# Two passes over the edges of a graph network: loops on the engines, or every quad written out

## The chip, the cores and the metric

The kernel runs on one core of one Trainium2 chip, in one launch. The metric is the device time of one execution in microseconds (us), lower is better. The engines go by their short names: PE (TensorE, its weight loads apart as PEld), DVE (VectorE), ACT (ScalarE), POOL (GpSimd) and SP (SyncE, which here only issues transfers). Each has its own stream of instructions, and they meet at semaphores.

## What is computed

Two layers of attention over a graph of 6250 nodes and 106,250 edges, each followed by a residual and a layer norm. The edges are sorted by destination. Cut to the work per edge:

```python
# layer 0: 8 heads of 16                       # layer 1: 4 heads of 32
Q, K, V = x @ Wq, x @ Wk, x @ Wv               x_src = x @ W_src + b_src; x_dst = x @ W_dst + b_dst
q = Q[dst] + rel_q[type]                       c = leaky_relu(x_src[src] + x_dst[dst] + emb[type], 0.2)
k = K[src] + rel_k[type] + time_emb @ Wt + bt  logits = einsum("ehd,hd->eh", c, att)
v = V[src] + rel_v[type]                       mx = segment_max(logits, dst)
euclid = sum(q * k, -1) / 4 * decay            ex = exp(logits - mx[dst])
dist = norm(m[src] - m[dst])                   attn = ex / segment_sum(ex, dst)[dst]
logits = a*euclid - (1-a)*beta*dist*decay      agg = segment_sum(x_src[src] * attn, dst)
ex = exp(logits - segment_max(logits, dst)[dst])   y = x + film(agg @ W_out + b_out)
agg = segment_sum(v * ex / segment_sum(ex, dst)[dst], dst)
x = norm(x + attention_block(agg))             x = norm(x + norm(y))
```

## The kernel before

The edges lie in tiles of 128, and nodes in blocks of 120. Where a tile spans two blocks it is worked through once for each, so there are 884 steps, and four steps make a quad: 221 quads with work (`sz.quads`; 224 by the padded count `NQUAD`). The program has six stages with barriers between them: `front` (schedule, tables), `edges0`, `join_tiles` with `nodes0`, `edges1`, `join_tiles`, `nodes1`. The change touches `edges0` and `edges1` alone.

In `edges0` every engine walks over the quads c = 0, 1, 2, ... in a function `emit` (on POOL `gather`). What one quad takes:

- POOL gathers the rows of the 4 x 128 source nodes with four indirect transfers (L1106) into a ring of 12 quads. It waits until the sums of the quad 12 before are made (L1103).
- PE multiplies the edge features (L1321), the queries (L1325) and the points (L1331, L1333), and, for the quad 8 before, the one-hot matrix with the weighted values (L1345, `sums`).
- DVE adds the times (L1161), multiplies by the queries (L1166), reduces per head (L1172), builds the transposed one-hot matrix of the quad 2 ahead (L1132) and the other one-hot matrix (L1180), scales the values (L1196), and adds four partial sums to the accumulator (L1150), whose block is read from a table into registers every fourth quad (a register load, L949). Once in four quads (a group, `LQ0`) it adds the distances (L1185, L1199) and one quad later makes the running maximum (L1190, L1204, L1211, L1215).
- ACT squares (L1283), copies the sums out of PSUM (L1275), and issues half of the feature loads; SP issues the rest and the loads by group.

`edges1` is built alike, with a ring of 16 quads, groups of eight, and a lag of ten quads between a quad's logits and its sums: POOL L1838, PE L2014, L2016 and L2040, DVE L1866 (transposed one-hot), L1879, L1884, L1888, L1895, L1898, L1908 (four adds), ACT L1981.

The order on each engine is that of the code. What the change concerns is how the quads are laid out in the program. Before, each engine has three stretches: a **head** written out, a **loop** whose body holds one turn of the ring, and a **tail** written out. In `edges0` the head is quads 0 to 23, the loop has 15 rounds of 12 quads (24 to 203), and the tail is the rest. In `edges1` the head is quads 0 to 31, the loop has 11 rounds of 16 quads (32 to 207). A loop of 15 rounds jumps back 14 times, and one of 11 rounds 10 times. In a body, the round is a register i, and each wait is for a number that depends on it; the helpers `nth0`, `group`, `slot` and `Chain.base` return a number where i is None and an expression of the register where it is not:

```python
def nth0(i, c, per=1, plus=0):
    v = c * per + plus
    return v if i is None else i * (RQ0 * per) + v
```

Of the kernel before, what the change touches and what calls it, by code (L numbers as in the profile page):

```python
# [39 lines left out]
LQ = 8  # L40
RQ = 16
# [3 lines left out]
LQ0, RQ0, LAG0, NQN = 4, 12, 7, 2  # L45
# [550 lines left out]
def tables0(nc, k, ctx):  # L596
# [4 lines left out]
    C = sz.steps // P  # L601
    PER = 2
    FROM = NGR - NBP // PER
    XT, FT = 6, 4
# [356 lines left out]
def edges0(nc, k):  # L961

    io, sz = k.io, k.sz
    NBP, S, T = sz.nbp, sz.steps, sz.tiles
    W = W0
    NQUAD = S // QS
    HEAD = 2 * RQ0
    NITER = (NQUAD - HEAD - LAG0 - 4) // RQ0
    TAIL = HEAD + NITER * RQ0
    PER = RQ0 * 7 + RQ0 // LQ0 * 5  # L970
    GS = LQ0 * QS
    BQ = 1
    with ExitStack() as ctx:
# [38 lines left out]
        vec = sem("vec")  # L1012
# [11 lines left out]

        def quads(i, c0, emit):
            for c in range(c0, c0 + (RQ0 if c0 else HEAD)):
                emit(i, c)

        def whole(eng, emit):
            quads(None, 0, emit)  # L1030
            with eng.Fori(0, NITER) as i:
                quads(i, HEAD, emit)
            for c in range(TAIL, NQUAD + LAG0 + 4):
                emit(None, c)

        with nc.Block() as block:
            @block.sync
            def _(sp):
# [50 lines left out]
                for c in range(5):  # L1089
                    load_feat(None, c)  # L1090
                whole(sp, emit)
                sp.wait_ge(zeroed, 64)
# [5 lines left out]
            def _(pl):  # L1098
# [11 lines left out]

                quads(None, 0, gather)
                with pl.Fori(0, NITER) as i:
                    quads(i, HEAD, gather)
                for c in range(TAIL, sz.quads):
                    gather(None, c)

            @block.vector
            def _(dve):
                V = nc.vector
                v = Chain(dve, vec)  # L1120
                V.memset(wbd[:, :, :], 0.0).then_inc(ready, 1)
                v.did(V.memset(acc, 0.0))
                count = {"base": v.n}
# [11 lines left out]
                def emit(i, c):  # L1135
                    w, a = c - LAG0, c - LAG0 - 2
                    v = Chain(dve, vec, count["base"] if i is None else i * PER + count["base"])
                    r = c % RQ0 * QS
# [84 lines left out]
                for j in range(k.sz.joins):  # L1223
                    if j % 16 == 0:
                        tiles = load_joins(nc, k, ET.DVE, 0, j, k.sz.etiles)
                    V.tensor_scalar(k.apart[:, j:j + 1], k.joinf[:, j:j + 1], k.entry[:, bass.ds(tiles[j % 16], 1)], None, ALU.subtract)
                quads(None, 0, emit)
                first = count["base"]
                with dve.Fori(0, NITER) as i:
                    quads(i, HEAD, emit)  # L1230
                assert count["base"] - first == PER, (count["base"] - first, PER)
                count["base"] = first + PER * NITER
                for c in range(TAIL, NQUAD + LAG0 + 4):
                    emit(None, c)

            @block.scalar
            def _(act):
# [65 lines left out]
                for c in range(5):  # L1303
                    load_feat(None, c)
                whole(act, emit)

            @block.tensor
            def _(pe):
# [52 lines left out]

                edge(None, 0)
                whole(pe, emit)


# [373 lines left out]
def edges1(nc, k):  # L1739

    io, sz = k.io, k.sz
    NBP, S = sz.nbp, sz.steps
    W = W1
    NQUAD = S // QS
    HEAD = 2 * RQ
    NITER = (NQUAD - HEAD) // RQ - 1
    PER = RQ * 6 + RQ // LQ * 2
    with ExitStack() as ctx:
# [32 lines left out]
        vec = sem("vec")  # L1781
        LAG = LQ + 2

        def quads(i, c0, emit):
            for c in range(c0, c0 + (RQ if c0 else HEAD)):
                emit(i, c)

        def whole(eng, emit):
            quads(None, 0, emit)
            with eng.Fori(0, NITER) as i:  # L1790
                quads(i, HEAD, emit)
            for c in range(NQUAD - RQ, NQUAD + LAG + 2):
                emit(None, c)
# [4 lines left out]
        with nc.Block() as block:  # L1798
            @block.sync
            def _(sp):  # L1800
# [21 lines left out]
                group_in(None, 0)  # L1822
                whole(sp, emit)
                chunks = math.ceil(sz.quads / 4)
# [4 lines left out]
            def _(pl):  # L1829
# [12 lines left out]

                quads(None, 0, gather)
                with pl.Fori(0, NITER) as i:
                    quads(i, HEAD, gather)
                for c in range(NQUAD - RQ, sz.quads):
                    gather(None, c)

            @block.vector
            def _(dve):  # L1850
                V = nc.vector
                v = Chain(dve, vec)
# [4 lines left out]
                pre = v.n  # L1857
# [10 lines left out]
                counted = {}  # L1868

                def emit(i, c):  # L1870
                    w, a = c - LAG, c - LAG - 1
                    g_u = c // LQ % 2
                    v = Chain(dve, vec, counted["base"] if i is None else i * PER + counted["base"])
                    if live(i, c + 2):
# [39 lines left out]
                    if maxing:  # L1914
                        u = m // LQ % 2
                        n = m // LQ // 2
# [17 lines left out]
                    if live(i, a):  # L1934
                        v.settle()
                        dve.sem_inc(added, 1)
                    counted["n"] += v.n
                    counted["base"] = counted["base"] + v.n

                counted.update(n=0, base=pre)  # L1940
                for c in range(2):
                    transposed_onehot(None, c)
                quads(None, 0, emit)
                first = counted["base"]
                counted["n"] = 0
                with dve.Fori(0, NITER) as i:
                    quads(i, HEAD, emit)
                assert counted["n"] == PER, counted["n"]
                counted["base"] = first + PER * NITER
                for c in range(NQUAD - RQ, NQUAD + LAG + 2):  # L1950
                    emit(None, c)

            @block.scalar
            def _(act):
# [41 lines left out]
                index(None, 0)  # L1996
                whole(act, emit)

            @block.tensor
            def _(pe):  # L2000
# [42 lines left out]

                edge(None, 0)
                whole(pe, emit)


# [431 lines left out]
```

## Time and profile before

| | us |
|---|---|
| median of 3 runs | 3325.63 |
| lowest, highest | 3320.14, 3325.68 |
| span of the profiled execution | 3808.8 |

The profile is of one execution, which took 483 us longer than the runs that were timed. Its span is split by the stages as follows: `front` 0 to 316, `edges0` to 1881, the first join to 1944, `nodes0` to 2231, `edges1` to 3655, and the last two to 3808.8. Over the whole span PE is busy 68%, DVE 65%, POOL 51%, ACT 30%; these shares mix six stages. "Idle" in a row of the timeline is the time before that instruction in which its engine did nothing, and behind the arrow stands what ended it: "issue" where the engine waited for nothing the profile shows, "remote" where a signal arrived whose giver had long been done. Register, branch and transfer-issuing instructions are not counted as busy. Each row of an engine with a "q" (DVEq, PEldq) is of its sequencer.

### The profile page before, as it was taken

The page shows a single profiled execution, that of the slowest core. Times are in us where ns is not written, and L with a number is a line of the kernel's source. Part 1 is how long each engine was busy: PE and PEld are TensorE (multiplying, and loading weights), DVE is VectorE, ACT ScalarE, POOL GpSimd, SP SyncE. Part 2 cuts the span into 40 slices and gives each one's busy share as a digit, 9 for nine tenths or more (in the row PEclk, how much of TensorE's full clock was granted, in tenths as well). Part 3 has the DMA queues.
Part 4 walks back from the last instruction along what each step waited for, and adds up shares of the span by engine and source line. Part 5 has one row for each costly group of instructions (what it writes and reads, how often), then busy time and mean ns, then how long its engine had stood idle before and what let it go on. Part 6 is the DMA issues. An engine that isn't in the chain of part 4 may idle for free. (4 is left out here: it accounts for less than half of the span.)

```text
span 3808.8 us, 60179 instructions
## 1 busy us (share of the span) xinstructions
PE 2583.3 (68%) x13302; PEld 1992.9 (52%) x13303; DVE 2475.7 (65%) x5935; ACT 1131.3 (30%) x3887; POOL 1924.7 (51%) x1957
## 2 busy tenths in 40 slices
PE   4893777777777777787668844666666566666654
PEld 3572555555555555565444423555555555555553
DVE  6443677677776767677755543666666666666678
ACT  2441444434343434444325520111111111111115
POOL 1004455555555555556330045666666666666554
PEclk9896888888888888898689977778788788878765
DMA  5475455555555555555301132333332333333221
GB/s 103 95 221 170 123 156 149 154 146 156 146 154 148 152 150 145 151 155 156 93 3 27 27 71 61 68 68 69 64 70 62 66 69 69 69 69 69 52 52 34
DMA packets 253667, 386.96 MB, mean 102 GB/s; under 512 B 70853, under 2 KB 168881, under 8 KB 249642
## 3 DMA queue, kind: packets, MB, share of 16 engines
q0 software_dynamic: 86432, 239.62, 24.7%
q1 hardware_dynamic: 132662, 130.96, 13.8%
q10 hardware_dynamic: 34260, 13.43, 1.4%
q14 instruction: 266, 2.18, 0.2%
q8 instruction: 47, 0.77, 0.1%
HBM read 342.88 MB, written 40.92 MB: 101 GB/s over the span
## 5 line engine op out<-in xcount | busy, mean ns | idle before, releaser
L1838 POOL DMA_INDIRECT pair<-d_table,e_idx x884 | 886.8, 1003 | 780.6 <-ACT e_idx L1962 300.6
L1106 POOL DMA_INDIRECT pair<-d_table,e_idx x884 | 870.5, 985 | 649.8 <-issue 238.6
L2040 PE MATMUL e_p_r<-pair,e_oh 128*122 128x132 f32 x1768 | 332.1, 342 | 425.5 <-DVE pair L1895 319.3
L1321 PE MATMUL e_p_t<-e_wbd,e_feat 128*128 128x512 f32 x442 | 289.1, 741 | 385.4 <-DVEq L1170 296.7
L2040 PEld LDWEIGHTS e_p_r<-pair,e_oh 128*122 128x122 f32 x1768 | 280.3, 233 | 467.3 <-issue 356.9
L1981 ACT COPY pair<-e_p_r 122x264 f32<-122x264 f32 x442 | 160.0, 380 | 994.2 <-DMA pair<-in_xT 471.9
L2014 PE MATMUL e_p_x<-pair,iden 128*128 128x264 f32 x884 | 342.8, 477 | 104.0 <-issue 63.2
L2016 PEld LDWEIGHTS e_p_x<-big,e_oht 128*128 128x128 f32 x1768 | 331.6, 232 | 48.9
L1325 PEld LDWEIGHTS e_p_q<-big,e_oht 128*128 128x128 f32 x1768 | 281.1, 226 | 136.5 <-issue 136.5
L1879 DVE SCALAR_TENSOR_TENSOR e_prod<-e_p_x,e_att 128x512 f32<-128x512 f32 x221 | 151.0, 683 | 271.6 <-remote 232.6
L2016 PE MATMUL e_p_x<-big,e_oht 128*128 x1768 | 325.6, 315 | 0.0
L1275 ACT COPY e_bound<-e_p_r 122x272 f32<-122x272 f32 x442 | 154.9, 387 | 512.6 <-remote 343.7
L1333 PEld LDWEIGHTS e_p_m<-big,e_oht 128*128 128x128 f32 x1768 | 240.2, 196 | 127.3 <-issue 127.3
L1283 ACT ACTIVATE e_p_m<-e_p_m 128x128 f32<-128x128 f32 x884 | 234.2, 265 | 205.1 <-ACT e_bound L1275 95.2
L1321 PEld LDWEIGHTS e_p_t<-e_wbd,e_feat 128*128 128x128 f32 x442 | 77.5, 219 | 406.3 <-issue 322.7
L1150 DVE TENSOR_TENSOR big<-big,e_bound 120x136 f32 x884 | 259.4, 293 | 36.5 <-issue 17.2
L1325 PE MATMUL e_p_q<-big,e_oht 128*128 x1768 | 279.1, 310 | 0.0
L1166 DVE TENSOR_TENSOR pair<-pair,e_p_q 128x512 f32<-128x512 f32 x221 | 150.5, 681 | 191.3 <-remote 187.5
L1908 DVE TENSOR_TENSOR big<-big,pair 120x132 f32 x884 | 217.6, 294 | 85.4 <-ACT pair L1981 39.9
L1161 DVE TENSOR_TENSOR pair<-pair,e_p_t 128x512 f32<-128x512 f32 x221 | 151.9, 687 | 183.9 <-issue 122.6
L1345 PE MATMUL e_p_r<-pair,e_oh 128*122 128x136 f32 x1768 | 251.7, 286 | 19.4 <-DVE pair L1196 10.1
L1331 PE MATMUL e_p_m<-pair,iden 128*128 128x512 f32 x442 | 256.9, 667 | 0.0
(362 smaller groups left out, 4518.6 us busy)
## 6 DMA issues: line engine op xcount, KB each, us to landing
pair<-d_table,e_idx POOLq DMA_INDIRECT x1768
e_node<-d_node SPq DMA_DIRECT2D x28, 960.0 KB
e_node<-d_node SPq DMA_DIRECT2D x111, 240.0 KB
d_table<-tab_kmv SPq DMA_DIRECT2D x54, 360.0 KB
e_feat<-in_edge_attr ACTq DMA_DIRECT2D x442, 16.0 KB
e_feat<-in_edge_attr SPq DMA_DIRECT2D x442, 16.0 KB
e_gate<-d_gate SPq DMA_DIRECT2D x84, 64.5 KB
d_decay<-pair SPq DMA_DIRECT2D x7, 512.0 KB, 4.1
```

Source lines behind the costliest of these rows:

```text
L1106: nc.gpsimd.indirect_dma_start(rows[:, c % RQ0 * QS + t, 0:3 * D], None, k.d_table0, bass.IndirectOffsetOnAxis(ap=idx[c // LQ0 % 3][:, c % ...
L1150: last = V.tensor_tensor(to, to, bound[a // BQ % 3][0:BN, a % BQ * QS + t, :].unsqueeze(1), ALU.add)
L1283: last = A.activation(p_m[c % 2][:, t, :], p_m[c % 2][:, t, :], ACT.Square, accum_out=d2[c // LQ0 % 3][:, c % LQ0 * QS + t:c % LQ0 * QS + ...
L1321: M(p_t[:, :, :].rearrange("p t d -> p (t d)"), feat[c % 6][:, :], wbd[:, :, :].rearrange("p t d -> p (t d)"), start=True, stop=True).then ...
L1325: last = M(p_q[:, t, :], oht[c % 3][:, t * P:(t + 1) * P], qm[:, bass.ds(of[t], 1), 0:D], start=True, stop=True)
L1331: M(m[:, :, :], k.iden[:, :], rows[:, r:r + QS, D:2 * D], start=True, stop=False)
L1333: last = M(m[:, t, :], oht[c % 3][:, t * P:(t + 1) * P], qm[:, bass.ds(of[t], 1), D:2 * D], start=False, stop=(t == QS - 1))
L1345: last = M(p_r[h][0:R_LAST + 1, t - 2 * h, 0:W], oh[w % 2][:, t, :], rows[:, w % RQ0 * QS + t, 2 * D:R0], start=True, stop=True)
L1838: nc.gpsimd.indirect_dma_start(rows[:, r, :], None, k.d_table1, bass.IndirectOffsetOnAxis(ap=idx[c // LQ % 2][:, c % LQ * QS + t:c % LQ * ...
L2014: M(x[:, 2 * h:2 * h + 2, 0:W], k.iden[:, :], rows[:, r + 2 * h:r + 2 * h + 2, :], start=True, stop=False)
L2016: last = M(x[:, t, 0:W], oht[c % 4][:, t * P:(t + 1) * P], xd[:, bass.ds(held["blocks"][(c - 1) % 4 * QS + t if c else t], 1), :], start=F ...
L2040: last = M(p_r[h][0:R_LAST + 1, t - 2 * h, 0:W], oh[w % 2][:, t, :], rows[:, w % RQ * QS + t, :], start=True, stop=True)
```

## The change

The loops go. On all five engines and in both passes the quads are written out one after the other from c = 0 to the end, and the register i is None everywhere. So the body is no longer shared by the rounds, no jump is left between quads, and each wait names a constant. The work of a quad, its order and its buffers stay. The diff, with what is alike in `edges1` left out:

```diff
-    HEAD = 2 * RQ0
-    NITER = (NQUAD - HEAD - LAG0 - 4) // RQ0
-    TAIL = HEAD + NITER * RQ0
-    PER = RQ0 * 7 + RQ0 // LQ0 * 5
...
-        def quads(i, c0, emit):
-            for c in range(c0, c0 + (RQ0 if c0 else HEAD)):
-                emit(i, c)
-
-        def whole(eng, emit):
-            quads(None, 0, emit)
-            with eng.Fori(0, NITER) as i:
-                quads(i, HEAD, emit)
-            for c in range(TAIL, NQUAD + LAG0 + 4):
+        def whole(emit):
+            for c in range(NQUAD + LAG0 + 4):
                 emit(None, c)
...
-                whole(sp, emit)
+                whole(emit)
...
-                quads(None, 0, gather)
-                with pl.Fori(0, NITER) as i:
-                    quads(i, HEAD, gather)
-                for c in range(TAIL, sz.quads):
+                for c in range(sz.quads):
                     gather(None, c)
...
-                    v = Chain(dve, vec, count["base"] if i is None else i * PER + count["base"])
+                    v = Chain(dve, vec, count["base"])
...
-                quads(None, 0, emit)
-                first = count["base"]
-                with dve.Fori(0, NITER) as i:
-                    quads(i, HEAD, emit)
-                assert count["base"] - first == PER, (count["base"] - first, PER)
-                count["base"] = first + PER * NITER
-                for c in range(TAIL, NQUAD + LAG0 + 4):
-                    emit(None, c)
+                whole(emit)
```

On DVE, at the end of the loop's body in `edges0` and the start of the next quad. Before, the last quad of the body (`ISA` and `REGISTER_ALU` are register instructions; L74 is where the wait on DVE's own count is worked out):

```order
L1132 TENSOR_SCALAR e_oht<-e_node,part 128x512 [waits e0_points]
L74 REGISTER_ALU
L1150 ISA [waits e0_vec]
L1150 TENSOR_TENSOR big<-big,e_bound 120x136
L1180 ISA [waits e0_sums]
L1180 TENSOR_TENSOR e_oh<-iota_f,code 128x488
L1196 TENSOR_TENSOR pair<-pair 128x4x128 [waits e0_spread]
L74 REGISTER_ALU
L1150 ISA [waits e0_vec]
L1150 TENSOR_TENSOR big<-big,e_bound 120x136
L1229 REGISTER_ALU [waits e0_vec]
L1229 COMPARE_AND_BRANCH
```

After the jump back the engine stands at the body's first instructions:

```order
L949 TENSOR_LOAD tile_block
L1159 ISA
L1160 ISA [waits gathered00]
L1161 TENSOR_TENSOR pair<-pair,e_p_t 128x4x128 [waits e0_times]
L1147 ISA
L74 ISA [waits e0_evicted]
L1150 ISA [waits e0_vec]
L1150 TENSOR_TENSOR big<-big,e_bound 120x136
```

The same place with the change (its lines stand 14 lower: L1118 is L1132, L1136 is L1150, L1147 is L1161):

```order
L1118 TENSOR_SCALAR e_oht<-e_node,part 128x512 [waits e0_points]
L1136 ISA [waits e0_vec]
L1136 TENSOR_TENSOR big<-big,e_bound 120x136
L1166 TENSOR_TENSOR e_oh<-iota_f,code 128x488 [waits e0_sums]
L1182 TENSOR_TENSOR pair<-pair 128x4x128 [waits e0_spread]
L1136 ISA [waits e0_vec]
L1136 TENSOR_TENSOR big<-big,e_bound 120x136
L949 TENSOR_LOAD tile_block [waits e0_vec]
L1147 TENSOR_TENSOR pair<-pair,e_p_t 128x4x128 [waits e0_times,gathered00]
L1136 ISA [waits e0_vec,e0_evicted]
L1136 TENSOR_TENSOR big<-big,e_bound 120x136
```

No work has moved. The branch with its register instruction is gone, the register load (L949) and the one `ISA` before each accumulator add, which places its block, have stayed, and the register instructions that worked out the waits are gone.

On POOL, at the start of the loop in `edges0`, before:

```order
L1106 DMA pair<-d_table,e_idx 128x384 x3
L1112 UNCONDITIONAL_BRANCH
L1112 ISA
L1103 ISA [waits e0_idx_in]
L1106 DMA pair<-d_table,e_idx 128x384 [waits e0_sums]
L1106 DMA pair<-d_table,e_idx 128x384 x3
L1103 REGISTER_ALU
```

and with the change (L1095 is L1106):

```order
L1095 DMA pair<-d_table,e_idx 128x384 x3
L1095 DMA pair<-d_table,e_idx 128x384 [waits e0_idx_in,e0_sums]
L1095 DMA pair<-d_table,e_idx 128x384 x3
L1095 DMA pair<-d_table,e_idx 128x384 [waits e0_sums]
L1095 DMA pair<-d_table,e_idx 128x384 x3
```

There too the gathers stand in the same order with the same waits, without the registers.

## Rows read from the trace of the kernel before

**Rows 1.** Busy time by stretch: its us, PE, PEld, DVE, ACT, POOL busy, clock, DMA, GB/s

```profile
316.00:1881.00 1565.00, 1161.63 (x6300) 874.47 (x6300) 1096.83 (x2614) 622.65 (x2602) 870.47 (x884) 0.86 0.52 145
...
2231.00:3655.00 1424.00, 855.01 (x4476) 751.08 (x4476) 910.24 (x2297) 184.44 (x555) 886.80 (x884) 0.79 0.31 65
...
2470.00:3552.00 1082.00, 675.23 (x3568) 594.69 (x3568) 714.16 (x1829) 145.76 (x442) 705.61 (x705) 0.81 0.32 68
```

**Rows 2.** Timeline of DVE, edges0, after jumps back 1, 6, 14: start, us, instruction, idle before

```profile
599.07 0.69 DVE L1161 TENSOR_TENSOR pair<-pair,e_p_t 128x512 f32<-128x512 f32 x1 [5.44 <-issue]
...
1007.14 0.69 DVE L1161 TENSOR_TENSOR pair<-pair,e_p_t 128x512 f32<-128x512 f32 x1 [4.96 <-issue]
...
1665.42 0.69 DVE L1161 TENSOR_TENSOR pair<-pair,e_p_t 128x512 f32<-128x512 f32 x1 [5.66 <-issue]
```

**Rows 3.** Timeline of DVE, edges0, quads of the tail (written out)

```profile
1757.41 0.68 DVE L1161 TENSOR_TENSOR pair<-pair,e_p_t 128x512 f32<-128x512 f32 x1
...
1767.66 0.69 DVE L1161 TENSOR_TENSOR pair<-pair,e_p_t 128x512 f32<-128x512 f32 x1 [1.37 <-issue]
...
1773.02 0.69 DVE L1161 TENSOR_TENSOR pair<-pair,e_p_t 128x512 f32<-128x512 f32 x1 [0.23 <-issue]
```

**Rows 4.** The branch on DVE by line, edges0: count, ns least/median/most, first and last

```profile
L1229 DVEq COMPARE_BRANCH  x15: 55/63/72, 593.8 to 1741.2; - x15
```

**Rows 5.** Instruction fetches in the loop of edges0, 517 to 1740: packets, MB, share

```profile
q14 instruction: 147, 1.20, 0.3%
q8 instruction: 4, 0.07, 0.0%
```

**Rows 6.** The same in the tail and drain of edges0, 1740 to 1881

```profile
q8 instruction: 5, 0.08, 0.3%
q14 instruction: 8, 0.07, 0.2%
```

**Rows 7.** Timeline of DVE, edges0, quads of the loop

```profile
1020.88 0.69 DVE L1161 TENSOR_TENSOR pair<-pair,e_p_t 128x512 f32<-128x512 f32 x1
...
1031.26 0.69 DVE L1161 TENSOR_TENSOR pair<-pair,e_p_t 128x512 f32<-128x512 f32 x1 [1.47 <-issue]
...
1037.66 0.69 DVE L1166 TENSOR_TENSOR pair<-pair,e_p_q 128x512 f32<-128x512 f32 x1 [5.50 <-remote]
```

**Rows 8.** Timeline of DVE, edges0, a quad of the head with the running maximum

```profile
443.43 0.69 DVE L1161 TENSOR_TENSOR pair<-pair,e_p_t 128x512 f32<-128x512 f32 x1 [0.22 <-DVE big L1150]
...
449.22 0.68 DVE L1161 TENSOR_TENSOR pair<-pair,e_p_t 128x512 f32<-128x512 f32 x1
```

**Rows 9.** DVE L1161 in all of edges0, columns as in rows 4

```profile
L1161 DVE TENSOR_TENSOR pair<-pair,e_p_t x221: 676/687/690, 368.2 to 1845.2; 128x512 f32<-128x512 f32 x111
```

**Rows 10.** Timeline of POOL, edges1: the first and the last of 25 gathers in a row

```profile
2269.52 0.94 POOL L1838 DMA_INDIRECT pair<-d_table,e_idx  x1 [0.30 <-issue]
...
2299.50 0.94 POOL L1838 DMA_INDIRECT pair<-d_table,e_idx  x1 [0.30 <-issue]
```

**Rows 11.** POOL L1838 in all of edges1, columns as in rows 4

```profile
L1838 POOL DMA_INDIRECT pair<-d_table,e_idx x884: 938/944/7592, 2236.0 to 3601.8; - x177
```

**Rows 12.** Timeline of POOL, edges0: the first gather after a jump back

```profile
812.77 0.94 POOL L1106 DMA_INDIRECT pair<-d_table,e_idx  x1 [0.30 <-issue]
```

**Rows 13.** Timeline of DVE, edges1: after the first and the last jump back

```profile
2572.97 0.49 DVE L1866 TENSOR_SCALAR e_oht<-e_node,part 128x512 f32<-128x512 bf16 x1 [3.49 <-issue]
...
2575.42 0.67 DVE L1884 TENSOR_TENSOR e_oh<-iota_f,code 128x488 f32<-128x488 f32 x1 [1.37 <-issue]
...
3457.89 0.49 DVE L1866 TENSOR_SCALAR e_oht<-e_node,part 128x512 f32<-128x512 bf16 x1 [3.18 <-issue]
```

**Rows 14.** Timeline of PE, edges0: a quad in the loop without idle time

```profile
994.98 1.02 PE L1321 MATMUL e_p_t<-e_wbd,e_feat 128*128 128x512 f32 x2
...
999.55 1.10 PE L1321 MATMUL e_p_t<-e_wbd,e_feat 128*128 128x512 f32 x2
```

More of the change, by code:

```diff
@@ L1304, in _ @@
                     load_feat(None, c)
-                whole(act, emit)
+                whole(emit)
             @block.tensor
@@ L1362, in _ @@
                 edge(None, 0)
-                whole(pe, emit)
+                whole(emit)
 class Weights0:
@@ L1744, in edges1 @@
     NQUAD = S // QS
-    HEAD = 2 * RQ
-    NITER = (NQUAD - HEAD) // RQ - 1
-    PER = RQ * 6 + RQ // LQ * 2
     with ExitStack() as ctx:
@@ L1782, in edges1, with whole @@
         LAG = LQ + 2
[L1784 to L1792, printed above, removed]
+        def whole(emit):
+            for c in range(NQUAD + LAG + 2):
                 emit(None, c)
@@ L1822, in _ @@
                 group_in(None, 0)
-                whole(sp, emit)
+                whole(emit)
                 chunks = math.ceil(sz.quads / 4)
@@ L1841, in gather @@
                             .then_inc(rows_in[c % RQ], 16)
[L1843 to L1846, printed above, removed]
+                for c in range(sz.quads):
                     gather(None, c)
@@ L1872, in emit @@
                     g_u = c // LQ % 2
-                    v = Chain(dve, vec, counted["base"] if i is None else i * PER + counted["base"])
+                    v = Chain(dve, vec, counted["base"])
                     if live(i, c + 2):
@@ L1936, in emit @@
                         dve.sem_inc(added, 1)
-                    counted["n"] += v.n
                     counted["base"] = counted["base"] + v.n
-                counted.update(n=0, base=pre)
+                counted.update(base=pre)
                 for c in range(2):
                     transposed_onehot(None, c)
[L1943 to L1951, printed above, removed]
+                whole(emit)
             @block.scalar
@@ L1996, in _ @@
                 index(None, 0)
-                whole(act, emit)
+                whole(emit)
             @block.tensor
@@ L2044, in _ @@
                 edge(None, 0)
-                whole(pe, emit)
+                whole(emit)
 def load_joins(nc, k, eng, which, j, bound):
```

## The prediction

> **What bounds the kernel now.** I read the split by stages first. The two passes take 1565 and 1424 us of the 3808.8 us span [rows 1], and the change touches nothing else; the other stages take 316 + 63 + 287 + 154 = 820 us together.
>
> Next comes DVE's timeline in `edges0`, from one start of L1161 to the next, which is one quad. Four quads in a row make a pattern. In the tail, a plain quad and the quad with the register load take 10.25 us together (1757.41 to 1767.66), and the next, with the distances, 5.36 us [rows 3]; the quad with the running maximum takes 5.79 us [rows 8]. That is 21.40 us for four, 5.35 us a quad, and in them DVE hardly idles: 0.23 us before L1161, and 1.37 us where the register load stands [rows 3]. POOL starts 25 gathers between 2269.52 and 2299.50, one in 1.249 us, so a quad of four costs it 5.00 us [rows 10]. PE takes 4.57 us a quad where it doesn't idle (994.98 to 999.55) [rows 14]. So DVE sets the pace of `edges0`, with POOL 0.35 us a quad behind it and PE 0.78.
>
> Then the quads that do not fit. Once in about four quads DVE stands for 5 to 6 us before L1166 until a signal arrives whose giver was long done (the last of the group) [rows 7]. I take these late signals for something that only the profiled execution has. Put together without them, `edges0` is 52 us until L1161 first starts (368.2 less 316), 220 x 5.35 = 1177, 36 from its last start to the stage's end (1881 less 1845.2) [rows 9], and 14 x 3.75 = 53 for the jumps back (below): 1318 us. `edges1` at POOL's pace is 5 us, 884 x 1.249 = 1104, and 53 after the last gather starts (3655 less 3601.8) [rows 10, 11]: 1162 us. With the 820 of the rest that is 3300 us, 25 below the median of 3325.6, while the span is 483 above it. Were the late signals real, the runs could not be that short.
>
> This also says who paces `edges1`. In its loop DVE is busy 714.16 us over 176 quads, 4.06 us a quad (the last of the group) [rows 1]; a register load adds 1.37 - 0.23 = 1.14 us every fourth quad [rows 3], 0.29 a quad, and the jumps back 0.29 (below). So DVE needs 4.64 us, under POOL's 5.00. At DVE's pace the pass would be some 80 us shorter and the sum 3220, much further from the median. I take POOL as its bound.
>
> **The change part by part.** (1) The jumps back of `edges0`. After one, DVE idles 5.44, 4.96 and 5.66 us before L1161 (the first, the sixth, the last) [rows 2], and over all fourteen of them 5.1 in the mean. In the tail the same place, with the same register load before it, costs 1.37 us [rows 3]. So a jump costs DVE 5.1 - 1.37 = 3.75 us. The branch itself lasts only 63 ns [rows 4]; the rest goes with fetches of instructions. In the loop there are 147 packets on the one instruction queue in 1223 us [rows 5], one in 8.3 us, and in the tail 8 in 141 us [rows 6], one in 17.6 us: the loop fetches its body again each round. DVE is the pace there, so nothing hides it: 14 x 3.75 = 52.5 us. What is late next is DVE's own work, then POOL. A round of twelve quads now takes 3 x 21.40 + 3.75 = 68.0 us, then 64.2; POOL's 12 x 5.00 = 60.0 stays under it, so POOL doesn't take the gain back.
>
> The Trainium skill, in Advanced Engine Details and Errata, section Control Flow Timing, gives a compare-and-branch about 108 ns. By that the 24 jumps would be worth 24 x 0.108 = 2.6 us and the change next to nothing; the trace's own branch agrees with it in size and the idle time behind it does not. The Trainium skill, in Runtime: NRT & Kernel Launch, section Instruction fetch mechanics, says that a taken branch to a place outside the current window of fetched instructions forces a transfer before execution goes on; by that rule the trace agrees with part 1.
>
> (2) The registers behind the waits. They run on the sequencers while the engine is still busy, so most cost nothing: that cover is the engine's own work, and it is gone only where DVE is idle. The plain quad and the one with the register load take 10.38 us in the loop (1020.88 to 1031.26) [rows 7] and 10.25 in the tail [rows 3]. The other two of four show no difference that I can see. So 0.13 us once in four quads: 45 x 0.13 = 6 us. The lower bound is 0, the upper 0.13 for each of the 180 quads, 23 us; I take 6, which is what the rows show.
>
> (3) The jumps back of `edges1`. DVE idles 3.49 and 3.18 us before L1866 (first and last of ten), and 1.37 once more before L1884 [rows 13]: about 4.7 us each, 47 in all, 4.7 / 16 = 0.29 a quad. POOL idles after a jump no more than between any two gathers, 0.30 us [rows 12], and has a ring of 16 quads to run ahead in. While POOL is the bound, DVE makes up 0.36 us in every quad and the 4.7 us are gone before the ring runs dry. I take 0; the bounds are 0 and 47.
>
> (4) PE, ACT, SP and POOL lose their jumps too. PE has 0.78 us of slack a quad and ACT and SP more, in both passes; 0. Their code is now fetched straight through. PE's queue of fetches brought 4 packets in the loop of `edges0` [rows 5], so its body was kept, and 5 in the far shorter tail [rows 6]. That is a cost from 0 up. I take 0, since the tail's quads, in which all engines fetch so, are the shortest of all [rows 3].
>
> The sum is 52.5 + 6 = 58.5 us. Against the profiled execution's own span that is 3808.8 - 58.5 = 3750; there the late signals stay, and part of the 47 of `edges1` may show as well, since POOL is not its bound there, down to 3703. The late signals are not in the timed runs, and neither part 1 nor part 2 rests on them, so the same us come off the median: 3325.6 - 58.5 = 3267 us.
>
> **The rivals.** *DVE paces `edges1` too.* Outside the profile the lag between a quad's logits and its sums may leave POOL waiting for `sums` rather than DVE for rows. Then the 47 us come on top: 3325.6 - 58.5 - 47 = 3220. For it: in the profile POOL is not back to back, 705.61 us busy of 1082 [rows 1]. Against: the sum of the stages.
>
> *The jump is cheaper when nothing is recorded.* If fetches wait behind the profiler's own traffic, a jump may cost DVE half, 1.9 us: 14 x 1.9 + 6 = 33, 3293. The rows can't exclude it.
>
> *Nothing changes.* A jump would then be worth its branch alone, 63 ns [rows 4], 14 of them under 1 us, and the 3.75 us would be the profile's, or the same fetches would stop DVE at the ends of its stretches of straight code instead. 3325. Against: in the tail no idle time before L1161 passes that of the register load by more than 0.2 us, over eight fetches [rows 3, 6].
>
> *Slower: PE is stopped by its own fetches.* It brought 5 packets for the some 25 quads of the tail [rows 6], one for about 5 quads; the 180 quads of the loop of `edges0` add 36 stops that its kept body didn't have. PE's slack over five quads is 5 x 0.78 = 3.9 us, so it decides from stops of 3.9 + 58.5 / 36 = 5.5 us. At two of DVE's stops, 7.5 us, the price is 36 x 3.6 = 130, net +71: 3397. Against: the same as above; for it: PE alone kept its loop.
>
> **How the numbers follow.** A measurement of this kernel tells about 0.2%, 6.6 us, from no change. Chances: forecast (3250 to 3285, the bounds of part 2 and some of part 3) 0.56; `edges1` as well (3200 to 3250) 0.20; the cheaper jump (3285 to 3319) 0.10; no change 0.08; slower 0.06. Faster 0.56 + 0.20 + 0.10 = 0.86. The range 3216 to 3308 holds the forecast, most of the second case and two thirds of the third, some 0.81.
>
> **What would show it.** In the changed kernel's profile no branch stands on DVE in either pass; the idle time before the line that was L1161 stays near 1.4 us where a round began; the plain quad takes 4.55 us; POOL's gathers stay 1.25 us apart; the packets of the queue that had 147 fall to near 80 over the same quads and PE's rise from 4 to about 40; the late signals stay. `edges0` shortens by 50 to 65 us and the span lies between 3700 and 3755. The prediction is wrong if DVE shows idle times of 2 us and more in straight code, if PE's idle time before L1321 grows, or if the timed runs gain over 80 us, which would mean that POOL does not bound `edges1`.

## The result, and the profile after

| | before | changed |
|---|---|---|
| median, us | 3322.89 (4 runs) | 3240.39 (4 runs) |
| lowest to highest | 3315.35 to 3325.68 | 3236.78 to 3244.62 |
| span of the profiled execution | 3808.8 | 3240.0 |

By the medians the changed kernel is 82.5 us faster. The ratio of the runs is 0.9769, with a 95% interval of 0.9751 to 0.9787, which is 77 us (71 to 83). The forecast was 3267, 58.5 us off; the time lies in its range of 3216 to 3308, and the gain is 24 us more than the sum by the medians, 12 to 24 by the interval.

One thing has to be said ahead, since no number can be read without it: all experiments below ran on three chips on which signals between engines arrive late in the two passes, in every profile taken there, and the timed runs are as long as the profiled ones. The profile of before looks like theirs and not like its own timed runs, so I take it to be from such a chip, though its chip is not recorded. The profile of the changed kernel (3240.0 us beside timed runs of 3237 to 3245) has no late signal. So the two spans in the table are not to be compared, and there is no profile of before on a chip without late signals.

First the changed kernel's busy time by stretch, which answers to [rows 1]: `edges0`, first join and `nodes0`, `edges1`, last two stages (us; PE, PEld, DVE, ACT, POOL busy; clock; DMA; GB/s):

```profile
316.00:1539.00 1223.00, 1043.61 (x6302) 799.87 (x6303) 1072.68 (x2613) 630.20 (x2600) 873.84 (x885) 0.98 0.67 186
1539.00:1892.00 353.00, 271.30 (x878) 142.96 (x875) 195.92 (x297) 154.74 (x252) 53.87 (x66) 0.91 0.13 35
1892.00:3086.00 1194.00, 792.61 (x4476) 697.32 (x4476) 905.62 (x2297) 193.16 (x555) 880.49 (x884) 0.85 0.36 78
3086.00:3240.00 154.00, 70.44 (x371) 58.85 (x371) 112.86 (x336) 58.28 (x204) 92.59 (x94) 0.59 0.27 53
```

In `edges0` DVE is busy 1073 of 1223 us. Its timeline shows one start of L1147 (which was L1161) per quad. Here are the quad where a round of twelve used to begin and the one after it, the next such place, and a plain quad later on with its successor:

```profile
1225.63 0.69 DVE L1147 TENSOR_TENSOR pair<-pair,e_p_t 128x512 f32<-128x512 f32 x1 [1.36 <-issue]
1230.92 0.69 DVE L1147 TENSOR_TENSOR pair<-pair,e_p_t 128x512 f32<-128x512 f32 x1 [0.22 <-DVE big L1136]
...
1289.95 0.69 DVE L1147 TENSOR_TENSOR pair<-pair,e_p_t 128x512 f32<-128x512 f32 x1 [1.35 <-issue]
...
1407.69 0.68 DVE L1147 TENSOR_TENSOR pair<-pair,e_p_t 128x512 f32<-128x512 f32 x1
...
1412.24 0.69 DVE L1147 TENSOR_TENSOR pair<-pair,e_p_t 128x512 f32<-128x512 f32 x1 [0.21 <-DVE big L1136]
```

Where a jump cost 5 us and more [rows 2], there is now the 1.36 us of the register load, as in the tail of before [rows 3]. Twelve quads take 1289.95 - 1225.63 = 64.3 us (64.2 was forecast), and the plain quad takes 4.55, as forecast.

Over all of `edges0`, for L1147: count, least, median and most ns, first and last start, and below it what ended DVE's idle time ahead of it (us, times). It answers to [rows 9]:

```profile
L1147 DVE TENSOR_TENSOR pair<-pair,e_p_t x221: 676/686/690, 341.0 to 1503.1; 128x512 f32<-128x512 f32 x111
  issue: 73.7, 54
  DVE big L1136: 24.0, 105
  PE e_p_t L1300: 4.0, 6
```

From the first to the last start are 1162.1 us for 220 quads, 5.28 each, and only 4.0 us ahead of L1147 are a wait for another engine: DVE paces this pass. POOL is close behind it. For its gathers in `edges0` the same view says (busy time 873.6 by the page):

```profile
L1095 POOL DMA_INDIRECT pair<-d_table,e_idx x884: 940/947/1447, 316.3 to 1488.1; - x177
  issue: 256.7, 818
  PE e_p_r L1324: 42.1, 64
```

Of the 1171.8 us from its first to its last gather POOL waits 42.1 for sums and is busy or between two gathers in the rest. So a still faster DVE could shorten this pass by about 42 us, an estimate from this row, before POOL is the pace here too.

In `edges1`, the same view for POOL's gathers, which answers to [rows 11], and two rows of the page: DVE's wait for the gathered rows, and PE's idle time in `edges0`:

```profile
L1807 POOL DMA_INDIRECT pair<-d_table,e_idx x884: 940/944/7834, 1897.1 to 3045.7; - x177
  ACT e_idx L1919: 304.3, 1
  issue: 254.1, 834
  PE e_p_r L1997: 14.9, 49
...
L1845 DVE SCALAR_TENSOR_TENSOR e_prod<-e_p_x,e_att 128x512 f32<-128x512 f32 x221 | 150.9, 683 | 197.2 <-PE e_p_x L1973 196.7
...
L1300 PE MATMUL e_p_t<-e_wbd,e_feat 128*128 128x512 f32 x442 | 240.3, 625 | 175.2 <-DVEq L1156 149.1
```

POOL's 304.3 us are the wait ahead of its first gather of the stage. After that it is busy 880.5 us (the page's sum for L1807), idles 254.1 between one gather and the next and waits 14.9 for sums: 1149.5, and 3045.7 - 1897.1 = 1148.6. POOL paces this pass in the changed kernel, and DVE stands 197 us waiting for what PE makes of the rows that POOL brings.

### The profile page after: what moved, and what is told of

Its sections match the earlier page's. It is cut to its first block and busy times, and to the rows that moved or that the text cites. A ratio compares the mean times of both kernels' runs of the same rounds, so it can differ in the third digit from the quotient of the medians.

```text
span 3240.0 us, 52340 instructions
## 1 busy us (share of the span) xinstructions
PE 2409.7 (74%) x13302; PEld 1869.6 (58%) x13302; DVE 2447.2 (76%) x5934; ACT 1148.3 (35%) x3886; POOL 1921.7 (59%) x1957
## 3 DMA queue, kind: packets, MB, share of 16 engines
q14 instruction: 166, 1.36, 0.1%
## 5 line engine op out<-in xcount | busy, mean ns | idle before, releaser
L1807 POOL DMA_INDIRECT pair<-d_table,e_idx x884 | 880.5, 996 | 573.3 <-ACT e_idx L1919 304.3
L1095 POOL DMA_INDIRECT pair<-d_table,e_idx x884 | 873.6, 988 | 306.6 <-issue 256.7
L1971 PE MATMUL e_p_x<-pair,iden 128*128 128x264 f32 x884 | 334.3, 465 | 316.9 <-issue 183.9
L1300 PE MATMUL e_p_t<-e_wbd,e_feat 128*128 128x512 f32 x442 | 240.3, 625 | 175.2 <-DVEq L1156 149.1
L1971 PEld LDWEIGHTS e_p_x<-pair,iden 128*128 128x128 f32 x884 | 157.7, 222 | 344.7 <-issue 250.2
L1973 PEld LDWEIGHTS e_p_x<-big,e_oht 128*128 128x128 f32 x1768 | 321.9, 226 | 44.0
L1997 PE MATMUL e_p_r<-pair,e_oh 128*122 128x132 f32 x1768 | 277.1, 306 | 82.8 <-DVE pair L1861 82.4
L1997 PEld LDWEIGHTS e_p_r<-pair,e_oh 128*122 128x122 f32 x1768 | 247.0, 209 | 104.1 <-DVE pair L1861 103.6
L1304 PEld LDWEIGHTS e_p_q<-big,e_oht 128*128 128x128 f32 x1768 | 233.9, 193 | 106.8 <-issue 106.8
L1136 DVE TENSOR_TENSOR big<-big,e_bound 120x136 f32 x884 | 260.3, 294 | 30.5 <-DVE e_lg L1185 14.3
L1304 PE MATMUL e_p_q<-big,e_oht 128*128 x1768 | 234.5, 276 | 0.0
L1312 PE MATMUL e_p_m<-big,e_oht 128*128 x1768 | 233.0, 275 | 0.0
L1324 PEld LDWEIGHTS e_p_r<-pair,e_oh 128*122 128x122 f32 x1768 | 225.7, 190 | 8.9 <-DVE pair L1182 8.9
L1147 DVE TENSOR_TENSOR pair<-pair,e_p_t 128x512 f32<-128x512 f32 x221 | 151.4, 685 | 101.7 <-issue 73.7
L1310 PE MATMUL e_p_m<-pair,iden 128*128 128x512 f32 x442 | 226.5, 594 | 0.0
```

The lines of the kernel that those rows point to most:

```text
L1095: nc.gpsimd.indirect_dma_start(rows[:, c % RQ0 * QS + t, 0:3 * D], None, k.d_table0, bass.IndirectOffsetOnAxis(ap=idx[c // LQ0 % 3][:, c % ...
L1136: last = V.tensor_tensor(to, to, bound[a // BQ % 3][0:BN, a % BQ * QS + t, :].unsqueeze(1), ALU.add)
L1300: M(p_t[:, :, :].rearrange("p t d -> p (t d)"), feat[c % 6][:, :], wbd[:, :, :].rearrange("p t d -> p (t d)"), start=True, stop=True).then ...
L1304: last = M(p_q[:, t, :], oht[c % 3][:, t * P:(t + 1) * P], qm[:, bass.ds(of[t], 1), 0:D], start=True, stop=True)
L1310: M(m[:, :, :], k.iden[:, :], rows[:, r:r + QS, D:2 * D], start=True, stop=False)
L1312: last = M(m[:, t, :], oht[c % 3][:, t * P:(t + 1) * P], qm[:, bass.ds(of[t], 1), D:2 * D], start=False, stop=(t == QS - 1))
```

## The experiments

On the three chips of the experiments the kernel before took 3774 to 3823 us. Each kernel was timed beside it on the same chip; the gain is (1 - ratio) times that chip's median of before, with the 95% interval. The texts of what was expected speak of differences of medians, which lie up to 7 us beside these.

| kernel | chip | median | before there | ratio (95%) | gain, us |
|---|---|---|---|---|---|
| edges0_straight | A | 3729.8 | 3781.6 | 0.9880 (0.9856 to 0.9903) | 45 (37 to 54) |
| edges1_straight | A | 3760.6 | 3781.6 | 0.9950 (0.9931 to 0.9969) | 19 (12 to 26) |
| dve_straight | A | 3756.1 | 3781.6 | 0.9940 (0.9919 to 0.9961) | 23 (15 to 31) |
| after_again | B | 3737.8 | 3823.0 | 0.9766 (0.9741 to 0.9791) | 89 (80 to 99) |
| edges0_straight_2 | B | 3739.7 | 3823.0 | 0.9771 (0.9753 to 0.9790) | 88 (80 to 94) |
| two_rounds | B | 3802.5 | 3823.0 | 0.9950 (0.9933 to 0.9967) | 19 (13 to 26) |
| others_straight | B | 3796.8 | 3823.0 | 0.9931 (0.9915 to 0.9947) | 26 (20 to 32) |
| edges0_straight_3 | C | 3722.8 | 3781.4 | 0.9847 (0.9806 to 0.9887) | 58 (43 to 73) |
| two_rounds_2 | C | 3769.1 | 3781.4 | 0.9960 (0.9937 to 0.9983) | 15 (6 to 24) |
| after_3 | C | 3688.1 | 3774.3 | 0.9754 (0.9723 to 0.9786) | 93 (81 to 105) |
| edges1_straight_2 | C | 3758.9 | 3774.3 | 0.9958 (0.9933 to 0.9982) | 16 (7 to 25) |

**The kernel before, profiled again** (no edit).

> The kernel before, unchanged, profiled a second time. The first profile has a span of 3808.8 us, 483 over the timed median, and signals that arrive 5 to 6 us late about once in four quads; the changed kernel's profile has neither (3240.0 us). Theory A: the late signals belong to one disturbed execution; then this profile has a span of 3320 to 3340 us, edges0 of some 1290 to 1320 us and no late signals. Theory B: they belong to the loops (register instructions under the profiler); then the span is 3750 to 3850 us again.

Its time was 3777.9 us, with a span of 3776.1, and the timed runs of the same kernel on that chip had a median of 3781.6. So neither theory held as it was put: the span is the one that theory B gave, but its cause is not the profiler, since there is no gap between span and runs, and not the loops alone, since the changed kernel has late signals on such chips too (next). The late signals are not one disturbed execution. They go with the chip.

**The changed kernel on such chips** (no edit).

> The changed kernel, unchanged, beside the kernel before, with the halves below on the same chip. On the chip of the first runs before took 3323 us and this one 3240; on another chip before took 3781 us, with signals 5 us late once in about four quads. Theory A: the late signals belong to that chip and hit this kernel too: there the gain is near the 52 + 21 us that its two halves gave, some 3705 us; on a chip without them 3240. Theory B: the changed kernel has none anywhere: 3240 us on any chip.

> The changed kernel, unchanged, beside its edges1 half on the same chip. On the chip of the first runs it took 82.5 us off, on one with halts 89. Expected again 80 to 90 us off, and more than the 45 to 87 that edges0 alone gave on three chips: the other half is to make up the difference.

Theory A held as to the signals: 3737.8 and 3688.1 us, and the changed kernel has late ones too. Its size did not: the gain is 89 us where 52 + 21 were added up from the halves on another chip. The gains of 89 and 93 us stand beside the 82.5 of the chip without late signals. What a late signal looks like, on DVE in the profile of after_3:

```profile
703.42 0.68 DVE L1147 TENSOR_TENSOR pair<-pair,e_p_t 128x512 f32<-128x512 f32 x1
708.08 0.69 DVE L1152 TENSOR_TENSOR pair<-pair,e_p_q 128x512 f32<-128x512 f32 x1 [3.76 <-remote]
```

From 704.8 to 708 no engine starts anything but POOL, whose gathers go on; PE had finished the queries that L1152 waits for. Only the two passes have waits of DVE that end in "remote"; the changed kernel on the chip without late signals has none anywhere. The same four stretches as above, of after_3:

```profile
316.00:1794.00 1478.00, 1127.88 (x6305) 841.51 (x6306) 1085.14 (x2614) 616.04 (x2600) 879.89 (x886) 0.92 0.55 154
1794.00:2145.00 351.00, 268.81 (x875) 141.27 (x872) 195.37 (x297) 154.69 (x252) 53.44 (x65) 0.91 0.13 36
2145.00:3540.00 1395.00, 849.84 (x4476) 748.71 (x4476) 906.06 (x2297) 186.14 (x555) 883.19 (x884) 0.78 0.31 67
3540.00:3694.00 154.00, 71.43 (x371) 59.53 (x371) 112.81 (x336) 58.27 (x204) 92.67 (x94) 0.58 0.30 53
```

The same program takes 1478 us in `edges0` instead of 1223, and 1395 in `edges1` instead of 1194, but 351 instead of 353 in the stages between and 154 in the last two on either chip.

**One pass alone.** The diff is that of the change, cut to the function `edges0`, or to `edges1`; of `edges0`:

```diff
-            quads(None, 0, emit)
-            with eng.Fori(0, NITER) as i:
-                quads(i, HEAD, emit)
-            for c in range(TAIL, NQUAD + LAG0 + 4):
+            for c in range(NQUAD + LAG0 + 4):
                 emit(None, c)
```

> Only edges0 is written out, edges1 keeps its loops. The prediction's sum says 52.5 + 6 = 58.5 us off the kernel before: some 3264 us beside 3323. If DVE also paces edges1, the whole gain of 82.5 us is shared out, and this kernel still gains 58.5 while the other half brings 24. Rival: the jump costs more than its idle time before L1161 shows, and all 82.5 us are here: some 3240 us.

> Only edges0 is written out. On the chip with the late signals it took 52 us off, where the prediction's sum says 52.5 + 6. On a chip without them: 3323 - 58.5 = 3264 us by the prediction's sum; if the lacking 24 us are in edges0, 3240.

> Only edges0 is written out. On the two chips with late signals it took 52 and 83 us off. On a chip without them: 58.5 us off by the prediction's sum (3264 us beside 3323), with the other 24 in edges1; or all 82.5 us here, 3240.

> Only edges1 is written out, edges0 keeps its loops. The prediction says 0 us (POOL bounds it and hides the ten jumps of 4.7 us): 3323 us. What is left of the measured gain after the predicted 58.5 is 24 us: if it is here, some 3299 us, which would be 2.4 us for each of ten rounds. If DVE set the pace of all of edges1, 47 us: 3276.

> Only edges1 is written out. The prediction says 0 us. The first run of this kernel took 19 us off (12 to 26). Theory A: POOL does not hide the ten stops of VectorE of 4.7 us entirely, a part near 2.4 us each is paid: 24 us off, and the halves add up to the whole. Theory B: what the first run showed was the registers in the halts of that chip; on a chip without halts 0 us off.

`edges0` alone gave 45, 88 and 58 us, `edges1` alone 19 and 16. On chip C, which has all three, the halves add up to 58 + 16 = 74 (49 to 98) beside 93 (81 to 105) for the whole. On chip B, which has `edges0` and the whole, they gained 88 (80 to 94) and 89 (80 to 99), which leaves 2 us (-14 to 19) for `edges1` there. So `edges1` by itself brings something on chips A and C, though far less than the 47 us of its stops, and most of the gain is in `edges0`. The scatter of `edges0` from chip to chip is larger than the intervals; I can't explain it.

Why the stops of `edges1` bring so little can be read off DVE's groups (us busy, mean ns, idle time ahead and what ended most of it). First the kernel before (before_again), L1866 being the place after a jump and L1879 the first to use what PE makes of the gathered rows, and then the same two in edges1_straight_2 (L1853 and L1866 there):

```profile
L1866 DVE TENSOR_SCALAR e_oht<-e_node,part 128x512 f32<-128x512 bf16 x221 | 110.8, 502 | 70.6 <-issue 48.5 <-DVE big L1908 15.3 <-remote 3.4
L1879 DVE SCALAR_TENSOR_TENSOR e_prod<-e_p_x,e_att 128x512 f32<-128x512 f32 x221 | 151.3, 685 | 215.9 <-remote 163.2 <-PE e_p_x L2016 26.5 <-issue 25.8
```

```profile
L1853 DVE TENSOR_SCALAR e_oht<-e_node,part 128x512 f32<-128x512 bf16 x221 | 114.6, 519 | 29.4 <-DVE big L1895 4.4 <-issue 2.3
L1866 DVE SCALAR_TENSOR_TENSOR e_prod<-e_p_x,e_att 128x512 f32<-128x512 f32 x221 | 150.9, 683 | 310.0 <-remote 289.1 <-PE e_p_x L1994 20.2 <-DVE big L1895 0.2
```

The idle time after jumps falls from 70.6 to 29.4 us, as it should; DVE's idle time before the next line grows from 215.9 to 310.0. What grows there is "remote", from 163.2 to 289.1, so on these chips DVE comes earlier to a place where it waits for a late signal. That POOL hides the stops is not what this shows: in before_again POOL itself waits 135.7 us for transfers and 76.1 for sums among its gathers of `edges1`, and so doesn't run without a break.

**Long rounds.** Loops and registers stay, but a loop has two rounds of 84 quads in `edges0` and two of 80 in `edges1`: 13 of 14 jumps back go, and 9 of 10.

```diff
-            for c in range(c0, c0 + (RQ0 if c0 else HEAD)):
+            for c in range(c0, c0 + (LONG * RQ0 if c0 else HEAD)):
...
-            with eng.Fori(0, NITER) as i:
-                quads(i, HEAD, emit)
+            with eng.Fori(0, 2) as i:
+                quads(i * LONG, HEAD, emit)
```

> Both passes keep loops with their registers, but a loop is two rounds of up to seven times the quads: 12 or 13 of the 14 jumps back in edges0 are gone and 8 or 9 of the 10 in edges1, and all register instructions behind the waits stay. The prediction's step 2 says that the registers are worth 6 us of the gain: then this kernel gains 82.5 - 6 less one jump of 3.75 us in edges0, some 3250 us beside 3323. Rival: the registers carry the 24 us that the sum lacks: some 3274 us.

> Both passes keep their loops and registers, but a loop is two rounds of up to seven times the quads, so that 12 or 13 of 14 jumps back in edges0 and 8 or 9 of 10 in edges1 are gone. On the chip with the late signals this gave 20 us where the whole change gave 85: the jumps would be a quarter of the gain there and the registers the rest. Theory A: the two chips differ, and register instructions are slow where signals are late; on a chip without late signals the predicted split holds: 82.5 - 6 - 4 = 72 us off, 3250 us. Theory B: the registers are the larger part on any chip: 20 us off, 3300 us.

The gain was 19 and 15 us, with the whole change at 89 and 93. Theory A was made for a chip without late signals and was not tried there, and theory B, "on any chip", wasn't either; on these chips the jumps by themselves bring about a fifth. DVE's groups of L1161 and L1166 (and their like) tell where a part of theirs went, first of before_again (chip A), then of two_rounds_2 (chip C):

```profile
L1161 DVE TENSOR_TENSOR pair<-pair,e_p_t 128x512 f32<-128x512 f32 x221 | 152.0, 688 | 183.6 <-issue 128.5 <-remote 39.5 <-DVE big L1150 10.5
L1166 DVE TENSOR_TENSOR pair<-pair,e_p_q 128x512 f32<-128x512 f32 x221 | 150.7, 682 | 165.1 <-remote 161.6 <-issue 1.9 <-PE e_p_q L1325 1.3
```

```profile
L1162 DVE TENSOR_TENSOR pair<-pair,e_p_t 128x512 f32<-128x512 f32 x221 | 151.8, 687 | 163.0 <-issue 78.0 <-remote 57.8 <-PE e_p_t L1321 17.4
L1167 DVE TENSOR_TENSOR pair<-pair,e_p_q 128x512 f32<-128x512 f32 x221 | 150.5, 681 | 175.0 <-remote 167.7 <-issue 3.8 <-PE e_p_q L1325 1.3
```

The part "issue" of L1161 falls from 128.5 to 92.6 in two_rounds and 78.0 in two_rounds_2: most of the stops after jumps are gone from DVE. But the waits for late signals ("remote") before the two lines are 241 and 226 instead of 201, so a good part is taken back. In after_3 (chip C) they stand at 228, with "issue" at 71.7:

```profile
L1147 DVE TENSOR_TENSOR pair<-pair,e_p_t 128x512 f32<-128x512 f32 x221 | 151.4, 685 | 233.4 <-remote 147.3 <-issue 71.7 <-PE e_p_t L1300 9.2
L1152 DVE TENSOR_TENSOR pair<-pair,e_p_q 128x512 f32<-128x512 f32 x221 | 150.0, 679 | 87.3 <-remote 80.8 <-issue 3.5 <-PE e_p_q L1304 2.3
```

The two lines together stand idle 338 us in two_rounds_2 and 321 in after_3, so they show only 17 of the 78 us between the two kernels on this chip. By the edits, what still differs between long rounds and straight code is one jump back in each pass and the registers behind the waits, so nearly all of the rest must be the registers. On these chips register instructions are at times slow. Least, median and most ns of one place of ACT in `edges0`, in before_again and then in after_3:

```profile
L1255 ACTq FUSED_REGOPS  x442: 16/43/728, 308.5 to 1797.6; - x148
```

```profile
L1234 ACTq FUSED_REGOPS  x442: 37/37/42, 315.4 to 1733.1; - x148
```

Counted over all records, 388 instructions of registers, waits and branches took 0.64 to 0.76 us in before_again (85 on DVE, 73 on ACT, 230 on SP; nearly all in `edges0`), 375 and 335 in the two runs with long rounds, 87 in after_again, 43 in after_3, and 3 in the changed kernel on the chip without late signals. An operation on registers takes DVE 40 ns as a rule, so 85 of them cost some 85 x 0.66 = 56 us of its sequencer's time, and the 17 in after_3 some 11. That is a price of registers that the prediction did not have; how much of it lies on the path was not measured apart. Two things speak for caution. The three runs with only `edges0` written out have 89, 80 and 81 such instructions and gained 45, 88 and 58 us, so the count alone doesn't make the gain. And the register operations of ordinary length, 3000 on DVE alone before and none after, may cost time wherever a late signal has left DVE idle and nothing covers them; no run tells the two apart.

**VectorE alone, and the others alone.** Written out are both passes on DVE only, or on PE, ACT, SP and POOL only. The edit of the first, in `edges0`:

```diff
-                quads(None, 0, emit)
-                with dve.Fori(0, NITER) as i:
-                    quads(i, HEAD, emit)
-                for c in range(TAIL, NQUAD + LAG0 + 4):
+                for c in range(NQUAD + LAG0 + 4):
                     emit(None, c)
```

> VectorE's code alone is written out, in both passes; the other four engines keep their loops. The prediction puts all of the gain on VectorE's path: the whole measured gain of 82.5 us, some 3240 us. If the jumps of PE, ACT, SP or POOL cost something once VectorE no longer stops, the gain is smaller: with half of the rounds' stops moved to another engine, some 3280 us.

> PE, ACT, SP and POOL are written out in both passes, VectorE keeps its loops. The prediction puts nothing on these four: 3323 us, no change. If their jumps cost time beside VectorE's, this kernel shows the 24 us that the sum lacks: 3299.

The times are 23 and 26 us shorter. But both of these kernels give a wrong output, off by 2.2%, where all the others give the right one. With one set of engines in loops and the other straight some value is not what it should be, though each wait is for the same number as in kernels that are right. Why is not known, so their times are a hint and no measurement of a part.

As a hint they say that, with late signals, DVE alone does not carry the gain. In the profile of dve_straight the part "issue" before L1161 is 44.9 us, where before_again on the same chip has 128.5, so the stops are gone; but "remote" before it is 81.1 instead of 39.5 and the wait for PE 33.4 instead of 5.2. DVE then waits for the engines that still stop. The two gains make 49 together and the whole change about 90, which would mean that each part brings more when the other is done; as one was taken on chip A and the other on chip B, and both kernels are wrong, that isn't shown.

## Why the prediction was right, and where it was not

**The jumps of `edges0`, 52.5 us: right in DVE's idle time; in device time it was not taken apart.** DVE's idle time "issue" before L1161 is 122.6 us in the profile of before and 128.5 in before_again, and 73.7 in the changed kernel: 48.9 and 54.8 less. It hardly depends on the chip (71.7 in after_3). In the changed kernel on the chip without late signals DVE paces the pass, and its waits before L1147 for other engines are 4.0 us in all. There each us of a stop should count, so I let the step stand, but no run on such a chip removed the jumps alone. Where signals are late they count for less: long rounds, which take nearly the same stops away, gave 15 to 19 us.

**The registers, 6 us (0 to 23): too low on chips with late signals, open on the other.** The whole change gains 70 to 78 us more than long rounds, which have lost nearly all the jumps too. I had read the price off two quads in a row; they say nothing of the register instructions that are slow now and then, nor of those that a late signal leaves without cover.

**The jumps of `edges1`, 0 us (0 to 47): not far off, for a reason that is shown only after the change.** 19 and 16 us were measured on two chips and next to nothing is left for them on a third, so a third of the stops or less showed. That POOL paces the pass is borne out by the changed kernel's rows on the chip without late signals (POOL's 1149.5 us above, with 14.9 of waits). On the chips with late signals POOL has breaks, and what took the stops' place there were waits for late signals. So the 16 to 19 us, with intervals from 7 to 26, say little about the chip of the result.

**The lacking 24 us (12 to 24 by the interval): open.** The sum is 58.5 and the medians give 82.5. `edges1` with 16 to 19 would make it 75 to 78 (the ratio of the runs gives 77); a higher price of the registers would do as well. On the chip without late signals neither half and no long rounds were run. That the time came out inside the range is sound for the part that DVE's idle time shows, and owed to the width of the range for the rest.

**The other engines, 0 us: right for `edges0` on the chip without late signals as far as its trace shows.** PE's idle time before L1300 is a wait for DVE, 149.1 of 175.2 us, and none of that row is "issue": PE's own fetches don't stop it there, and the slower rival is out. In `edges1` 183.9 us of PE's idle time before the line that was L2014 do stand under "issue", and whether fetches are among them is open; but POOL waits only 14.9 us for PE there, so it costs little. Over the 180 quads of the old loop (456.6 to 1417.9 us) the fetches are:

```profile
q8 instruction: 48, 0.79, 0.3%
q14 instruction: 78, 0.64, 0.2%
```

They were 4 and 147 [rows 5]; about 40 and 80 were forecast. With late signals the 0 is in doubt: the kernel with these four engines written out was 26 us shorter, though its output is wrong.

**"I take these late signals for something that only the profiled execution has": wrong.** They are in every profile on three chips, whose timed runs are as long. Two sentences hang on this step. "The late signals stay" and "the span lies between 3700 and 3755" failed for the profile of the changed kernel (3240.0 us) and hold for the chips that have them (3745.9 in after_again; 3694.2 in after_3, just below).

**The rebuild of the stages, 3300 us, agreed by cancelling errors.** It was to show what a run without late signals looks like; its parts can now be held against the changed kernel. The rebuild less the gain makes `edges0` 1318 - 58.5 = 1260 us, which is 1223: its start is 25 us (341.0 less 316), not 52, and a quad 5.28, not 5.35. It makes `edges1` 1162, which is 1194. There a gather takes 996 ns in the mean, where I had taken a stretch of 25 gathers for all 884: the mean distance is 1148.6 / 883 = 1.301 us and not 1.249, which is 46 us more, and the end after the last gather starts is 40 us (3086 less 3045.7) and not 53. The rest is 823, not 820. So errors of -37, +32 and +3 us nearly cancel, and the rebuild less 58.5 is 3241.5 beside the span of 3240.0. That also says that the 24 us which the gain has too much are the 25 which the rebuild lacked against before: a cost of the loops that neither had, unless errors cancel there too. The rebuild was my main reason for POOL's pacing `edges1`; the conclusion was right for the changed kernel, the reason weak. So was the test I set at the end, that a gain over 80 us would mean that POOL does not bound `edges1`: the gain is 82.5, and POOL bounds it.

**The branch and the fetch.** The Trainium skill, in Advanced Engine Details and Errata, section Control Flow Timing, gives a compare-and-branch about 108 ns. By that figure alone, an estimate, the change would have been worth 2.6 us. The trace's branch lasts 63 ns [rows 4], and the 48.9 to 54.8 us that went with 14 jumps are 3.5 to 3.9 us each.

## What to carry to other kernels

Price a loop on an engine by the idle time behind the jump, not by the branch, and then ask which engine paces the stage. Here 14 stops of 3.75 us went from DVE's idle time in full where DVE was the pace, and ten of 4.7 us were worth some 16 to 19 us in a pass that waited for something else. Expect the stops to turn into other waits: where signals were late, taking nearly all jumps away gave 15 to 19 us. A sum of stages rebuilt from a short stretch of rows can agree with the measured time by cancelling errors; use the mean over all instructions of the group (busy plus idle, first to last start), and cut two profiles at the same event, before you lean on a difference of 25 us. Where a profile's span is far from the timed median, ask whether the profile is from another chip before you call the difference an artefact, and measure a split of the gain on the chip that the split is meant for.

## What the runs showed of the hardware

The same program took 3240 us on one chip and 3688 to 3738 on others, and before 3323 against 3774 to 3823, with the difference in the two passes only (1478 against 1223 us, 1395 against 1194), while the other stages are alike (351 against 353, 154 against 154). In these passes PE, DVE and ACT at times all stand still together while POOL goes on: in after_3 for more than 2.5 us 19 times in the 1430 us of the gathers of `edges0` and 34 times in the 1340 us of those of `edges1`, and in the changed kernel on the chip without late signals once and 11 times. Single register instructions on DVE, ACT and SP take 0.7 us instead of some 40 ns, nearly all of them in `edges0`; in `edges1` after_3 has none of these, and yet that pass is 201 us longer there, so they are not what makes it long. Both passes have POOL issuing gathers nearly without a break and the other stages do not; whether that is the cause was not tried, nor what differs between the chips. Straight code has fewer register instructions to be hit, 43 and 87 slow ones instead of 388, which fits that the change is worth at least as much there.
